# Moving the transposes' evictions of a four-batch AdaLN layer: chunk 0 ahead of the last K/V tile's norms, chunk 3's transposes behind the fourth Q chunk

## What is computed

```
mod = silu(c) @ wmod                        # shifts, scales and gates, per batch
h   = layernorm(x) * (1 + ca) + sa
Xn  = layernorm(h) * gamma + beta
Q, K, V = Xn @ W_in + b_in ;  K, V rotated
A   = 0.5 * sum over rows(K/|K| * V/|V|) + 0.5        # one value per feature and batch
x   = x + ga * ((A * Q) @ W_out + b_out + h)
h   = layernorm(x) * (1 + cb) + sb
x   = x + gb * (relu(h @ W_up) @ W_down + (sum of softmaxed top-2 logits) * (h @ W_expert))
```

## Time and profile before

| | |
|---|---|
| median of 3 runs | 385.92 us (385.58 to 386.85) |
| time of the profiled execution | 386.43 us |
| span of its trace | 384.6 us |
| TensorE matmuls busy | 367.0 us (95%), 1664 matmuls |
| VectorE, ScalarE, GpSimd busy | 255.4, 166.7, 113.3 us |
| mean granted TensorE clock | 0.982 of 2.4 GHz |

### The profile page before, as it was taken

One profiled execution on the slowest core, in us unless ns is written; L12 is line 12 of the kernel. 1 busy time (PEld: TensorE's weight loads), 2 busy tenths in 40 slices (PEclk: granted clock), 3 DMA queues, 4 the chain that ended last, 5 costly groups with the idle time before them and its releaser, 6 DMA issues.

```text
span 384.6 us, 4649 instructions
## 1 busy us (share of the span) xinstructions
PE 367.0 (95%) x1664; PEld 286.9 (75%) x1664; DVE 255.4 (66%) x515; ACT 166.7 (43%) x293; POOL 113.3 (29%) x110
## 2 busy tenths in 40 slices
PE   4997999899997999989999999999999999999996
PEld 0155888678885888868788878888788878887885
DVE  0677799869978488876887559727550855084354
ACT  1337388884427821075314681247114612541210
POOL 0114683276932528425163151910000001000000
PEclk9988899999999899999999999999999999999999
DMA  7995964050030000000000002100200110011002
GB/s 222 378 388 191 348 258 168 0 164 2 2 82 2 0 0 2 27 2 2 0 27 2 0 0 111 28 2 27 82 2 0 55 56 0 0 57 55 2 0 109
DMA packets 10951, 27.42 MB, mean 71 GB/s; under 512 B 1185, under 2 KB 1569, under 8 KB 9777
## 3 DMA queue, kind: packets, MB, share of 16 engines
q1 hardware_dynamic: 10928, 27.13, 19.8%
HBM read 22.90 MB, written 4.23 MB: 71 GB/s over the span
## 4 chain that ended last, share of the span: by engine, by line
PE 66%; DVE 12%; issue 7%; ACT 6%; DMA 4%; POOL 2%; SPq 1%; DVEq 0%; ACTq 0%; POOLq 0%
PE ps L1032 19%; PE ps L1034 19%; PE ps L1033 19%; PE ps L1039 3%; PE ps L1056 2%; DMA xs<-in_wmod 2%; DMA xs<-in_X 2%; ACT sqj L444 2%; DVE hb L657 1%; PE ps L1047 1%; ACT ps L493 1%; DVE ps L690 1%; PE ps L1159 1%; PE ps L1160 1%; ACT t_hi L495 1%
## 5 line engine op out<-in xcount | busy, mean ns | idle before, releaser
L1032 PE MATMUL ps<-w_hi,t_hi 128*128 128x512 f32 x192 | 75.7, 394 | 0.0
L1034 PE MATMUL ps<-w_hi,t_lo 128*128 128x512 f32 x192 | 75.2, 392 | 0.0
L1033 PE MATMUL ps<-w_lo,t_hi 128*128 128x512 f32 x192 | 75.2, 392 | 0.0
L1032 PE MATMUL ps<-t_hi,w_hi 128*128 128x512 f32 x128 | 51.6, 403 | 0.0
L1032 PE MATMUL ps<-w_hi,g_hi 128*128 128x512 f32 (+1 forms) x132 | 51.3, 389 | 0.3 <-DVE g_lo L743 0.3
L1034 PE MATMUL ps<-w_hi,g_lo 128*128 128x512 f32 (+1 forms) x132 | 50.6, 383 | 0.0
L1033 PE MATMUL ps<-w_lo,g_hi 128*128 128x512 f32 (+1 forms) x132 | 50.5, 383 | 0.0
L1034 PE MATMUL ps<-t_hi,w_lo 128*128 128x512 f32 x128 | 50.4, 393 | 0.0
L1033 PE MATMUL ps<-t_lo,w_hi 128*128 128x512 f32 x128 | 50.4, 393 | 0.0
L683 DVE TENSOR_TENSOR t_lo<-ps,t_hi 128x512 fp32r<-128x512 f32 x32 | 21.8, 688 | 32.9 <-ACT t_hi L495 32.6
L1032 PEld LDWEIGHTS ps<-w_hi,t_hi 128*128 128x128 f32 x192 | 36.5, 190 | 7.6
(11 more groups left out here) (130 smaller groups left out, 613.8 us busy)
## 6 DMA issues: line engine op xcount, KB each, us to landing
xs<-in_X SPq DMA_DIRECT2D x4, 1024.0 KB, 7.5
stage<-in_w SPq DMA_DIRECT2D x4, 1024.0 KB, 6.8
out<-xs SPq DMA_DIRECT2D x15, 256.0 KB, 2.0
xs<-in_wmod SPq DMA_DIRECT2D x3, 1024.0 KB, 9.8
xs<-in_wmod SPq DMA_DIRECT2D x8, 256.0 KB, 7.0
stage<-in_w SPq DMA_DIRECT2D x8, 256.0 KB, 9.6
gate_bc<-mod_rows SPq DMA_DIRECT2D x8, 256.0 KB, 6.7
gate_bc<-in_wmod SPq DMA_DIRECT2D x1, 1024.0 KB, 11.9
```

The lines of the kernel that those rows point to most:

```text
L1032: mm(dst, l_hi, r_hi, start=start, stop=False)
L1033: mm(dst, l_hi, r_lo, start=False, stop=False)
L1034: return mm(dst, l_lo, r_hi, start=False, stop=stop)
```

## The change

It makes three edits in the attention part:

- ScalarE: E(0) moves from behind `norm_sums(b, 3)` (and, for b = 3, behind `split_hi(5)`) to the place in front of `norm_sums(b, 3)`.
- VectorE: S(0) moves from behind `kv_products(b, 3)` to between `kv_rows(b, 3)` and `kv_products(b, 3)`.
- TensorE: T(3) moves from behind Q chunk 2 to behind Q chunk 3. T(2) stays behind Q chunk 2.

No instruction is added or removed, and the same three edits apply to all four batches.

```diff
@@ scalar: attention(b)
                     normalise(b + 1, 2, 2)
                 else:
                     normalise(B, 0, NT)
+                t_evac(b + 1, 0)
                 norm_sums(b, 3)
                 if b == B - 1:
                     split_hi(5)
-                for c in range(NC):
+                for c in range(1, NC):
                     t_evac(b + 1, c)
                 if b + 2 < B:
                     normalise_x(b + 2)
@@ vector: attention(b)
                 kv_sum(b, 2)
                 kv_rows(b, 3)
+                t_split(b + 1, 0)
                 kv_products(b, 3)
-                t_split(b + 1, 0)
                 t_split(b + 1, 1)
                 kv_sum(b, 3)
                 a_pairs(b)
@@ tensor: attention(b)
                     if c == 1:
                         transposes(b + 1, 0)
                         transposes(b + 1, 1)
-                    if c == 2:
-                        transposes(b + 1, 2)
-                        transposes(b + 1, 3)
+                    if c >= 2:
+                        transposes(b + 1, c)
                 a_sums(b)
```

## The result

| | before | changed |
|---|---|---|
| first comparison, median | 385.75 us (4 runs) | 389.27 us (4 runs, 388.9 to 391.1) |
| ratio, 95% interval | | 1.0101 (1.0057 to 1.0145) |
| second comparison, median | 386.14 us (34 runs) | 388.81 us (12 runs) |
| ratio, 95% interval | | 1.0067 (1.0043 to 1.0091) |
| profiled execution, its span | 386.43, 384.6 us | 389.14, 387.3 us |

The changed kernel is slower, as forecast. The first comparison gives 3.5 us, the second, with more runs, 2.7 us. The second ratio's interval holds the forecast's 1.006 (388.2 to 385.92), and the first one's does too, but only at its lower end.

What follows compares the result with a forecast made beforehand. TensorE, busy 95% of the span, was taken as the bound. Terms 1.7 - 1.9 - 1.3 + 2.5 + 1.2 = +2.2 on 386.43 gave 388.6, or 388.2 us on the median; range 386.6 to 389.6.

Steps and rivals of the forecast that it cites:

- Batch 0, +1.7: End of batch 0: later T(3) delays S(3), normalise_x(2) and the Q evictions, a loss of 1.7 us reaching the next boundary.
- The rival that slack swallows it: Slack in the vector chain between 86 and 117 us absorbs batch 0's 1.7 us; kernel not slower, 385.2 to 386.5; chance 0.14.
- the path that the forecast named: Batch 0: T(3) later, so S(3) 1.70 us later, then x_shift(2), normalise_x(2), Q evictions and the last Q split.
- One sign: Output rows of batch 0: TensorE would wait about 0.6 us for each of the four Q splits.
- Batch 1, -1.9: End of batch 1: a_sums 3.2 us sooner, capped to a 1.9 us gain; 0.6 if the half-clock stretch was not typical.
- The cap itself: Batch 1: normalise_x(3) holds ScalarE from 126.05 to 128.9, so the Q chain allows only 1.9 of 3.2 us.
- Batch 2, -1.3: End of batch 2: a gain of 1.3 us if ab_col gets through at GpSimd's second addition's end, otherwise 0.45.
- the margin: Batch 2: ab_col issued 0.1 to 0.2 us in front of the end of GpSimd's second addition, taken as enough to get through.
- Batch 3, +2.5: End of batch 3: E(0) stands in front of norms and split_hi(5), so a_sums starts 2.5 us later.
- The clock at batch 3, +1.2: Batch 3: TensorE's idle time brings a fall to half clock, priced between nothing and 1.56 us, taken as 1.2.

Runs made afterwards that it cites:

- e2_middle: The three edits for batches 1 and 2 only, batches 0 and 3 as in the kernel before: 383.30 us against 386.14 before, ratio 0.9925.
- e4: Kernel before with only T(3) moved behind the fourth Q chunk, in all batches; E(0) and S(0) unmoved: 390.62 us against 386.40, ratio 1.0119.
- e8: The unchanged kernel before, traced once more: 49.0 us from T(0) of batch 1 to that of batch 2, against 50.3 in the profiled execution.
- e1: The three edits for batches 0, 1 and 2, batch 3 as in the kernel before: 384.99 us against 386.14 before, ratio 0.9990.
- e7: Kernel before with all edits at batch 2, and at batch 1 only E(0) and S(0) moved ahead: 383.06 us against 386.40, ratio 0.9917.
- e5_evictions_only: Kernel before with only E(0) and S(0) moved ahead, in all batches; T(3) stays behind Q chunk 2: 389.22 us against 386.40, ratio 1.0064.
- e3: Changed kernel with split_hi(5) at batch 3 put in front of E(0): 385.36 us against 386.14 for the kernel before, ratio 0.9983.
- e0_again: The changed kernel run once more, nothing altered: 388.81 us against 386.14 for the kernel before, ratio 1.0067.

## Why the prediction came out as it did

**Batch 0, +1.7: right.** 49.95 instead of 48.4, +1.6. The first Q eviction moved from 11.05 to 12.65 behind T(0), and all of it reached batch 1. The rival that slack swallows it falls with e2_middle. By e4 the late T(3) alone brings all of it, which is the path that the forecast named. One sign came out smaller: TensorE's waits for the Q splits in the output rows are shown with 0.3 us, three times, where about 0.6 was forecast four times; the last of them still ends 18.6 behind T(0), as forecast (87.5 - 68.80 = 18.7).

**Batch 1, -1.9: the step that failed, by its size.** The path was right; the term of the sum was not. Against the profiled execution it is exact (50.3 to 48.35). But that execution had a stretch at half clock there, and e8 shows the same code without it: 49.0, a gain of 0.65. I had written that the gain would be down to 0.6 should the stretch not have been typical, and then took the whole. The deficits give an estimate of how typical it is: 6.85 us for the kernel before and 5.8 for the three variants that keep batch 3 as it was and change batch 1 (e1, e2, e7), a difference of 1.05. One such fall is 1.7 us of deficit (granted clock 0.79 over the 8 us from 122 to 130), so some six executions in ten had it, if the rest of the program falls as often in both. Of the 1.57 us that it adds in front of `a_sums` (11.27 to 9.70), 1.3 reach the next batch (50.3 to 49.0). The term should have been about -0.65 - 0.6 x 1.3, about -1.5, as a mean, and -0.65 without a fall. The cap itself, `normalise_x(3)` on ScalarE, was right: 129.25 to 132.08, and e7_mix lifts it.

**Batch 2, -1.3: right**, 48.4 to 47.1. `ab_col` got through. VectorE:

```profile
178.46 0.23 DVE L740 TENSOR_TENSOR ab_col<-a_col,col 128x4 f32<-128x4 f32 x1
```

and GpSimd's additions, the second of which ends at 176.16 + 2 x 1.25 = 178.67:

```profile
176.16 5.01 POOL L356 TENSOR_TENSOR hb<-hb,bo_bc 128x512 f32<-128x512 f32 x4 [2.70 <-DVE pair L733]
```

It was issued 0.21 in front of that end, and took 0.23 instead of the 1.30 of the earlier trace rows. The instruction was thus held until that end and not longer, where I had placed the margin at 0.1 to 0.2. My reason for it was weaker than I thought. The instruction at 88.22 takes 0.28 also where none of these additions runs (changed kernel, 219.61), and the addition ended 0.17 behind its start: a hold until that end could not have shown in it. What decides is how far in front of an end the instruction is issued. In e5_evictions_only it came 0.03 in front at batch 1 and 0.01 at batch 2, and took 1.33 and 1.28, through the whole next addition. The Trainium skill (GPSIMD Engine Reference, Specifications) has the two engines contend for SBUF whenever VectorE reads two SBUF inputs; the trace agrees that it can, and shows what it costs: the remainder of the running addition, or the whole next one where it comes within 0.03 us of an end, so from nearly nothing to 1.3 us.

**Batch 3, +2.5: right**, 8.1 to 10.75, and 2.7 up to the end of the span, with `split_hi(5)` at 219.23 and E(1) at 221.03, where 219.2 and 221.05 were forecast. Of this e3 gives 1.1 to the weight; the remaining 1.5 is the late T(3) (e4: 9.65).

**The clock at batch 3, +1.2: near the mean, shown in two traces of four.** It was a choice between 0 and 1.56; the four traces have 0, 0, 1.6 and 3.0, and four are few.

**Sum.** With batch 1 at its mean: 1.6 - 1.5 - 1.3 + 2.6 + 1.2 = +2.6, and the 12 runs of e0_again give +2.7. The forecast's terms add up to +2.2 (388.2 against 385.92 is +2.3), so on the mean the batch 1 term is what it lacked. Against an execution with no fall at either place it is 1.6 - 0.65 - 1.3 + 2.6 = +2.25, as in the table; that this lies so near the forecast is luck, for there two errors, the fall counted at batch 1 and the fall counted at batch 3, cancel. The further 0.8 us of the first comparison I put down to its four runs: their mean deficit is 7.5 us, against 6.8 in the 12 of e0_again, and the 1.7 us in front of T(0) of batch 0 lie in untouched code. What makes the clock fall there in one execution and not in another stayed open.

## What to carry to other kernels

Ask of each reordered instruction what it waits for and what stands behind it on its engine: E(0) was moved in front of work that was ready, and at batch 3 ScalarE idled 5.9 us with that work behind it. An edit that applies to every turn of a loop is costed at every turn: at batches 1 and 2 it gained, at the first and last it lost more, and used only where it gains (e2_middle, e7_mix) it beats the kernel before by 0.8%. A wait removed on TensorE counts only up to the next thing that is late, here the eviction chain behind the last transposes.

## What the runs showed of the hardware

The same wait pattern, 1.33 and 0.62 us of idle around four transposes, was followed by half clock in one execution and by full clock in another of the same program, worth 1.6 us up to `a_sums`. The mean clock of the same kernel's runs lay between 0.977 and 0.987, which is up to 4 us of its time (384.1 to 389.2 over 34 runs), so a gain taken from one profiled execution has to be corrected for the falls that this execution happened to have. From T(0) of batch 3 to the end, the same changed kernel took 171.4, 173.0 or 174.4 us, by whether and how long the clock fell behind 1.95 us of idle. Eight superfluous matmuls in that gap cost no time (171.5). And a VectorE addition of four columns with both inputs in SBUF took 0.16 us where no GpSimd addition ran, 0.23 when issued 0.21 in front of the end of one, and 1.3 when issued 0.01 to 0.03 in front.
